# GRU and block attention on one core: the order of the first transfers, and how the bias and the constants get in

## The reference

```python
def cell(h, x):                       # 64 times; h [32, 512]
    gi = x @ W_ih + b_ih              # [32, 1536]
    gh = h @ W_hh + b_hh
    r = sigmoid(i_r + h_r); z = sigmoid(i_z + h_z)
    n = tanh(i_n + r * h_n)
    return (1 - z) * n + z * h
x = x + gru(cond, x)                  # [32, 64, 512]
blocks = x.reshape(32, 8, 8, 512).sum(2)
keys = rms_norm(blocks @ Wk.T) * rms_weight
attn = softmax(keys @ cond[1])
out = layernorm(x + (attn @ blocks) @ Wo.T) * ln_gamma + ln_beta
x = x + out
```

## Time and profile before

| | us |
|---|---|
| median of 3 runs | 377.51 (377.33 to 377.56) |
| the profiled execution | 377.32 |
| its span | 375.5 |
| TensorE busy | 362.8 (97%) |
| VectorE busy | 261.3 (70%) |
| ScalarE busy | 159.3 (42%) |
| GpSimd busy | 21.6 (6%) |

### The profile page before, as it was taken

The page is one execution under the profiler, slowest core; times in us unless marked ns, Lnnn a source line. Parts: engine busy times, 40 slices in busy tenths (PEclk is TensorE's granted clock), DMA queues, the critical chain, the costliest instruction groups (busy, mean ns, idle before and its releaser), DMA issues.

```text
span 375.5 us, 9832 instructions
## 1 busy us (share of the span) xinstructions
PE 362.8 (97%) x3285; PEld 213.5 (57%) x3285; DVE 261.3 (70%) x1132; ACT 159.3 (42%) x506; POOL 21.6 (6%) x55
## 2 busy tenths in 40 slices
PE   7999999999999999999999999999999999997894
PEld 4465555665655566666555666655556666334562
DVE  3725667777676778686768767676778676778785
ACT  4702226262534344352526262534344464756210
POOL 7002000000000000000000000000000000100230
PEclk9999999999999999999999999999999999999998
DMA  5975535323232322324141323232332322110047
GB/s 180 404 295 120 162 96 158 100 70 100 73 98 70 90 62 64 98 57 111 43 105 41 98 70 98 70 98 70 84 79 59 92 61 81 38 42 21 11 172 276
DMA packets 27485, 38.64 MB, mean 103 GB/s; under 512 B 2988, under 2 KB 19016, under 8 KB 27464
## 3 DMA queue, kind: packets, MB, share of 16 engines
q1 hardware_dynamic: 27432, 38.36, 35.4%
q10 hardware_dynamic: 32, 0.01, 0.0%
HBM read 18.17 MB, written 4.19 MB: 60 GB/s over the span
## 4 chain that ended last, share of the span: by engine, by line
PE 89%; DVE 6%; POOL 1%; issue 1%; DMA 1%; ACT 0%; DVEq 0%; POOLq 0%; SPq 0%
PE gates_ps L607 43%; PE gi_ps L575 37%; DVE gcx L1098 1%; POOL w_hh L376 1%; PE first_ps L607 1%; PE first_ps L668 1%; PE fourth_ps L607 1%; PE third_ps L607 1%; PE keys_ps L607 1%; PE fourth_ps L668 1%; PE third_ps L668 1%; PE keys_ps L668 1%; DMA h_tok<-hist 1%; DVE w_hh L1021 1%; PE gi_ps L589 1%
## 5 line engine op out<-in xcount | busy, mean ns | idle before, releaser
L607 PE MATMUL gates_ps<-w_hh,turned 128*32 128x384 f32 x1920 | 167.3, 489 | 0.5 <-DVE turned L829 0.5
L607 PEld LDWEIGHTS gates_ps<-w_hh,turned 128*32 128x32 f32 x1920 | 56.4, 109 | 85.5 <-issue 56.5
L575 PE MATMUL gi_ps<-w_ih_hi,xt_hi 128*128 128x384 f32 x240 | 87.2, 363 | 0.0
L575 PE MATMUL gi_ps<-w_ih_hi,xt_lo 128*128 128x384 f32 x240 | 81.2, 338 | 0.0
L575 PE MATMUL gi_ps<-w_ih_lo,xt_hi 128*128 128x384 f32 x240 | 80.2, 334 | 0.0
L489 ACT ACTIVATE rz<-gates_ps 128x256 f32<-128x256 f32 x60 | 23.1, 385 | 128.9 <-PE gates_ps L607 128.8
L893 DVE TENSOR_TENSOR rz<-gates_ps,rz 128x128 f32<-128x128 f32 x60 | 17.5, 292 | 79.6 <-ACT rz L489 79.6
L575 PEld LDWEIGHTS gi_ps<-w_ih_hi,xt_hi 128*128 128x128 f32 x240 | 45.0, 187 | 37.5 <-issue 36.9
L575 PEld LDWEIGHTS gi_ps<-w_ih_lo,xt_hi 128*128 128x128 f32 x240 | 45.1, 188 | 0.0
L575 PEld LDWEIGHTS gi_ps<-w_ih_hi,xt_lo 128*128 128x128 f32 x240 | 45.0, 187 | 0.0
L829 DVE STREAM_TRANSPOSE turned<-hist 128x32 f32<-128x32 f32 (+1 forms) x192 | 36.7, 216 | 2.2
(11 more groups left out here) (221 smaller groups left out, 302.5 us busy)
## 6 DMA issues: line engine op xcount, KB each, us to landing
gi<-gi_tok SPq DMA_DIRECT2D x60, 192.0 KB, 3.4
x1t<-in_x_t_dram SPq DMA_DIRECT2D x16, 256.0 KB, 3.1
gcx<-in_x_tok_dram SPq DMA_DIRECT2D x16, 256.0 KB, 3.2
h_tok<-hist SPq DMA_DIRECT2D x64, 64.0 KB, 2.2
out_dram<-gcx SPq DMA_DIRECT2D x16, 256.0 KB, 2.2
gcx<-in_w_ih_dram SPq DMA_DIRECT2D x4, 768.0 KB, 7.5
w_hh<-in_w_hh_dram SPq DMA_DIRECT2D x4, 768.0 KB, 8.9
wo_t<-in_wo_t_dram SPq DMA_DIRECT2D x1, 1024.0 KB, 5.4
```

The source lines that it names most:

```text
L575: mm = pe.matmul(gi_ps[tok][:, 0:G3], a[:, k, :], w[:, k, gi_cols(j)], start=(k == 0 and a is xt_hi and w is w_ih_hi), stop=(k == NJ - 1 a ...
L607: mm = pe.matmul(gates_bank(t)[j * B:(j + 1) * B, P:], before[:, k * B:(k + 1) * B], chunk(w_hh, k, j), start=False, stop=(k == NJ - 1), s ...
```

## The change

The three bias transfers, the four constant transfers, the selection matrices, the layout matmuls and the copies after them are gone. x and W_ih's first quarter are SP's first transfers, without a wait. Third is one broadcast transfer of the bias into all partitions: its source pattern is [4 chunks, 32 copies, 768 values], its destination [128 partitions, 768]. h0 comes after W_ih's last quarter, and x of the next four steps before it. VectorE adds the two biases of r and z, and then adds the bias to each of the four banks in PSUM when TensorE has finished the first quarter's matmuls there (`first_laid`); TensorE's second quarter waits for each bank (`first_seeded`). Seven warming matmuls stand where three stood. gamma, cond's row and rms_weight come in three broadcast transfers behind `b_hh_rz`; GpSimd forms the products `wq` and `wq_rec`. The gi chunk before step 0 takes its lo parts of W_ih last (`lo_last`), with a wait for each quarter, and `split_x` comes before the last quarter. The transpose of beta goes from step 0 to step 3. The copy of wq after step 0 is gone. `br_all` and `br_t` are one block smaller.

```diff
+                if last:
+                    sp.wait_ge(wq_ready, 2)
...
-            sp.wait_ge(bias_made, 1)
-            sp.dma_start(bias_rows[0:NJ, 0:G3], b_ih_d).then_inc(bias_in, 16)
-            sp.dma_start(bias_rows[NJ:2 * NJ, P:3 * P], b_hh_d[0:2 * D].rearrange("(j n) -> j n", j=NJ)
-                         ).then_inc(bias_in, 16)
-            sp.dma_start(bias_rows[NJ:2 * NJ, 3 * P:], b_hh_d[2 * D:].rearrange("(j n) -> j n", j=NJ)
-                         ).then_inc(bias_in, 16)
             sp.dma_start(x1t[:, 0], x_t_d[:, 0:NJ, :]).then_inc(x_first_in, 16)
             load_w_ih(0)
-            sp.dma_start(hist[:, S - 1, :], cond_d).then_inc(h0_in, 16)
+            sp.dma_start(bias_in_rec, bias_d[:, None, :].broadcast_to([NJ, B, 6 * P])).then_inc(bias_in, 16)
             load_w_ih(1)
             load_w_ih(2)
+            load_x_t(1)
             load_w_ih(3)
-            load_x_t(1)
+            sp.dma_start(hist[:, S - 1, :], cond_d).then_inc(h0_in, 16)
...
+            sp.dma_start(recs[:].rearrange("p c u -> p (c u)"), recs_d[:, None, :].broadcast_to([NJ, B, 4 * P])
+                         ).then_inc(consts_in, 16)
+            sp.dma_start(tok_consts[:].rearrange("p c n -> p (c n)"), rows_d[None, 0:2 * D].broadcast_to([P, 2 * D])
+                         ).then_inc(consts_in, 16)
+            sp.dma_start(rms_tok, rows_d[None, 2 * D:].broadcast_to([P, D])).then_inc(consts_in, 16)
             move_gi(0, -1)
...
+            pool.wait_ge(consts_in, 48)
+            pool.tensor_tensor(wq, wq, rms_tok, ALU.mult).then_inc(wq_ready, 1)
+            pool.tensor_tensor(wq_rec, wq_rec, rms_rec, ALU.mult).then_inc(wq_ready, 1)
...
-            act.activation(bias_rec, first_ps[0][:], ACT.Copy).then_inc(bias_kept, 1)
-            act.wait_ge(bias_kept, 1)
-            act.wait_ge(pe_warmed, Q)
-            for t in (1, 3):
-                act.activation(first_ps[t][:], bias_rec, ACT.Copy).then_inc(first_seeded, 1)
             for k in range(NJ):
+                if k == NJ - 1:
+                    act.wait_ge(pe_warmed, Q + 1)
+                    split_x(1)
                 act.wait_ge(w_ih_in[k], 16)
                 act.activation(w_ih_hi[:, k, :], w_stage[:, k, :], ACT.Copy).then_inc(w_hi_ready, 1)
...
+                order = [(k, a, w) for k in range(NJ) for a, w in terms]
+                if lo_last:
+                    order = [(k, a, w) for a, w in (terms[0], terms[2], terms[1]) for k in range(NJ)]
+                for m, (k, a, w) in enumerate(order):
+                    if lo_last and w is w_ih_lo:
+                        pe.wait_ge(w_lo_ready, k + 1)
...
-                if first and s == 0:
-                    lay_pick(small_ps, 2)
...
-            keep_warm(2)
-            pe.wait_ge(pick_made, 4)
-            pe.wait_ge(bias_in, 48)
-            pe.matmul(first_ps[0][:], own_rows, bias_rows, start=True, stop=True).then_inc(bias_laid, 1)
-            pe.wait_ge(pick_made, 5)
-            pe.wait_ge(wq_row_ready, 1)
-            pe.matmul(gi_ps[0][:, 0:3 * P], own_rows, const_rows[:, 0:3, :], start=True, stop=True
-                      ).then_inc(consts_laid, 1)
-            lay_pick(gi_ps[1], 0)
-            keep_warm(1).then_inc(pe_warmed, 1)
+            keep_warm(7).then_inc(pe_warmed, 1)
...
                 for t in range(Q):
-                    if k == 0 and t == 0:
-                        pe.wait_ge(bias_kept, 1)
-                    if k == 0 and t == 1:
-                        pe.wait_ge(first_seeded, Q - 1)
+                    if k == 1:
+                        pe.wait_ge(first_seeded, t + 1)
                     for j in range(NJ):
...
+                    if k == 0:
+                        mm.then_inc(first_laid, 1)
...
-            dve.memset(const_rows, 0.0).then_inc(rows_made, 1)
-            dve.memset(bias_rows, 0.0).then_inc(bias_made, 1)
...
-            dve.tensor_copy(first_ps[2][:], bias_rec).then_inc(first_seeded, 1)
+            dve.wait_ge(bias_in, 16)
+            dve.tensor_tensor(bias_rec[:, P:3 * P], bias_rec[:, P:3 * P], bias_in_rec[:, D:], ALU.add
+                              ).then_inc(bias_summed, 1)
+            dve.wait_ge(bias_summed, 1)
+            for t in range(Q):
+                dve.wait_ge(first_laid, t + 1)
+                dve.tensor_tensor(first_ps[t][:], first_ps[t][:], bias_rec, ALU.add).then_inc(first_seeded, 1)
+            split_w(0)
+            split_w(1)
+            split_x(1)
+            split_w(2)
             dve.wait_ge(h0_in, 16)
             for c in parts:
                 dve.transpose(turned[:, S - 1, c], hist[:, S - 1, c]).then_inc(ht_ready, 1)
-            for k in range(NJ):
-                split_w(k)
-            split_x(1)
+            split_w(3)
```

More of the change, by code:

```diff
@@ L66, in gru_block_attention @@
         scalar_warm = sb("scalar_warm", [P, 1])
[L68 to L71, removed]
+        tok_consts = sb("tok_consts", [P, 2, D])
+        gamma_tok, wq = tok_consts[:, 0, :], tok_consts[:, 1, :]
+        recs = sb("recs", [P, 4, P])
+        gamma_rec, beta_rec, wq_rec, rms_rec = (recs[:, c, :] for c in range(4))
         beta_t = sb("beta_t", [P, P])
@@ L314, in _ @@
         def _(pool):
[L315 to L324, removed]
             pool.memset(ident[:], 0.0).then_inc(made, 1)
@@ L503, in step @@
                 quad = i * 2 + s // Q - 1
-                if peeled and s == 0:
-                    act.wait_ge(consts_laid, 3)
-                    act.activation(wq[:], small_ps[:], ACT.Copy).then_inc(consts_kept, 1)
+                if peeled and s == S - 1:
                     act.wait_ge(beta_turned, 1)
@@ L639, in keep_warm @@
                 return mm
-            def lay_pick(bank, c):
-                for j in range(NJ):
-                    mm = pe.matmul(bank[:, j * P:(j + 1) * P], pick[:, j, :], const_rows[:, c, :],
-                                   start=True, stop=True)
-                mm.then_inc(consts_laid, 1)
-            keep_warm(2)
-            pe.wait_ge(pick_made, 4)
-            pe.wait_ge(bias_in, 48)
-            pe.matmul(first_ps[0][:], own_rows, bias_rows, start=True, stop=True).then_inc(bias_laid, 1)
-            pe.wait_ge(pick_made, 5)
-            pe.wait_ge(wq_row_ready, 1)
-            pe.matmul(gi_ps[0][:, 0:3 * P], own_rows, const_rows[:, 0:3, :], start=True, stop=True
-                      ).then_inc(consts_laid, 1)
-            lay_pick(gi_ps[1], 0)
-            keep_warm(1).then_inc(pe_warmed, 1)
+            keep_warm(7).then_inc(pe_warmed, 1)
             pe.wait_ge(x_first_in, 16)
@@ L1138 @@
     b_hh = by_chunk(inputs["L0_cond_b_hh"], (0, 1, 2))[0]
+    b_ih = by_chunk(inputs["L0_cond_b_ih"], (2, 0, 1)).reshape(NJ, G3)
+    rms, gamma, beta = (inputs[f"L1_cond_{name}"] for name in ("rms_weight", "ln_gamma", "ln_beta"))
     laid_out = {
@@ L1144 @@
         "w_ih": by_chunk(inputs["L0_cond_W_ih"], (2, 0, 1)).reshape(D, 3 * D), "w_hh": inputs["L0_cond_W_hh"],
-        "b_ih": by_chunk(inputs["L0_cond_b_ih"], (2, 0, 1)).reshape(NJ, G3),
-        "b_hh": _np.concatenate([b_hh[:, 0:2].reshape(-1), b_hh[:, 2].reshape(-1)]),
-        "rms_weight": inputs["L1_cond_rms_weight"],
+        "b_ih": b_ih,
+        "b_hh_rz": b_hh[:, 0:2].reshape(-1),
+        "bias": _np.concatenate([b_ih, b_hh[:, 2], b_hh[:, 0], b_hh[:, 1]], axis=1),
+        "recs": _np.concatenate([a.reshape(NJ, P) for a in (gamma, beta, cond[1], rms)], axis=1),
+        "rows": _np.concatenate([gamma, cond[1], rms]),
         "wk_t": inputs["L1_cond_Wk"].transpose(1, 0), "wo_t": inputs["L1_cond_Wo"].transpose(1, 0),
-        "gamma": inputs["L1_cond_ln_gamma"], "beta": inputs["L1_cond_ln_beta"],
     }
```

78 lines of the change are left out of this document (28 added, 50 removed).

## The result

Beside each other on one chip, the changed kernel took 383.21 us (median of 6 runs, 381.19 to 384.84), the kernel before 377.75 (6 runs, 377.33 to 378.43): a ratio of 1.0142 with a 95% interval of [1.0121, 1.0162]: slower. The forecast was 376.8 with a range of 374.8 to 378.2: the sign was wrong. The profiled execution took 382.63 us, of which the span is 380.6, 5.1 longer than before.

A forecast was written before the change was run, and what follows sets the result against it. TensorE's unbroken matmul run was taken as the bound, with matmuls and bytes as equal walls at the start. +0.15 for step 0 and -0.89 for `lay_pick` gave -0.74 us: 376.8 us, range 374.8 to 378.2.

The forecast's parts named there:

- Earlier first transfers: At the start: x and all transfers go out 2.55 us earlier, and TensorE begins real work at 6.6 instead of 9.38.
- The bias broadcast: Ahead of w_ih's second quarter: four DMA engines carry 98.3 KB each at 25.4 GB/s, 3.87 us, delaying later transfers on them.
- The clock: Rival: TensorE's idling before w_ih's second quarter drops its clock to half; +2.0 us, 379.5 in all; chance 0.08.
- the straggler: Rival: the slowest DMA engine at the start is one of the bias's four; w_hh lands at 25.4, 378.0 us; chance 0.12.
- +0.15 for step 0: End of step 0: w_hh's last quarter lands at 24.2, so the step ends at 25.1 against 24.93; matmul wall alike.
- Removed `lay_pick`: Between step 0's chunk and step 1: this matmul work leaves the chain, -0.89 us, whole.
- Bias adds hidden: VectorE's bias sum and four PSUM adds, 3.2 us, end before TensorE's second quarter needs them; cost 0, hidden by 1.5 us.
- Constants at no cost: Constants queued behind b_in and b_hh_rz, 1.05 MB, end near 32.7, first wanted in step 3; cost 0, cover 1.5 us.
- b_in is late: Rival: constants mix with b_in before step 1; each 1 us beyond the cover costs up to 1 us; 379; chance 0.07.
- The rival of sixteen engines: At the start: sixteen engines carry the bias in 0.97 us, step 0 ends 1.58 earlier, -2.47 in all, 375.0; chance 0.20.

## Why the prediction was wrong

- **Earlier first transfers: right.** x went out at 0.74 (forecast 0.71), w_ih's first quarter was in by 5.6 (5.5). TensorE began at 5.91, sooner than my 6.6, and was done with the first quarter at 8.73, not 9.6, since the full clock came during the warming. That made the idle stretch longer.
- **The bias broadcast: the step that failed, by size.** The engine count was right: four. The price was not. The prediction took 98.3 KB on each of four engines at 25.4 GB/s, 3.87 us; measured were 12.27 - 5.58 = 6.7 us from w_ih's first quarter to VectorE's sum. Two things were assumed and untrue. First, that an engine with more rows keeps its rate: alone, four engines in blocks of 32 partitions moved 21 GB/s each, and 15.5 beside the other transfers. Second, that the twelve others don't notice: all sixteen together moved 233 GB/s at a share of 0.92. So w_ih's second quarter came at 13.95, not 12.1.
- **The clock: a rival with chance 0.08, and it happened.** Its mechanism was right: TensorE idled 5.22 us. A mean of 0.98 over 5 to 12 us is a half clock for the last 0.2 to 0.3 of them, so the clock had been full for some 3 us of idling when it fell, much as at the end of the kernel before. It cost 2.3 us, against 2.8 forecast; in the four other executions where it fell in this place (two engines, distinct rows, VectorE's additions, blocks of eight) the same stretch cost 1.6, 1.7, 2.6 and 3.0. The chance hung on the transfer's rate, which I had taken as certain: the 2.5 us of forecast idling were only 0.6 less than what had come before the fall in rows 8, and only the straggler was allowed to lengthen them.
- **+0.15 for step 0: measured +4.27**, 2.01 from the late quarter and 2.3 from the clock. w_hh's last quarter was no wall any more, because the matmuls were later than it.
- **Removed `lay_pick`: right**, -0.90 against -0.89.
- **Bias adds hidden: right in the change**, although the cover shrank: with the bias at 12.27, bank 0's addition was over at 13.4, 0.5 us before TensorE could use it. With four transfers in blocks of eight the additions were what TensorE waited for.
- **Constants at no cost: right in the change, for the wrong reason.** It seems to hold there because everything else is late. With sixteen engines, b_in mixed with the constants and cost 1.2 us: the mechanism of the rival "b_in is late".
- **Not seen:** GpSimd's additions now ran beside the state update of step 0 (0.64), 0.40 at the loop's first return, and 0.7 in the end phase, where the granted clock is 0.58 in 349:353. The last shows up in some other kernels' executions too, also in one with a fast start (constants issued in step 2), and neither in the one with warming matmuls nor in the one with VectorE's additions to the change. So it isn't shown to belong to the change; its cause stays open, as does that of the 0.40.
- **The rival of sixteen engines** gave 375.0 for a kernel that measured 376.89; it had the gain of the start (step 1 3.10 us earlier, 2.47 forecast) and lacked the b_in stall.

What stays open: why few engines beside the full streams drop to 15 to 17 GB/s and slow the rest. That their rows cross the parts of SBUF that the other engines are writing would fit the two runs with blocks of eight partitions, and two engines at 25.5 GB/s alone, but beside the streams four blocks of eight gained only some 1.5 us. Which share is whose wasn't separated.

## What to carry to other kernels

Here a broadcast whose pattern began with four went over four DMA engines, one with two over two, and the weights behind it came late (13.95 and 19.21); with 32 or 128 first they came at 9.6 to 9.7. So give both sides a first dimension that is a multiple of 16, as a larger tensor in DRAM or as several transfers. Where TensorE waits early for a landing, price the clock as well as the wait: here 2.01 us of lateness brought 2.3 us of half clock. Before constants are moved behind a critical transfer, ask what waits for the last byte of that transfer, and put them after it by program order in time, not by place in the queue.

## What the runs showed of the hardware

- With nothing else in flight, four DMA engines in blocks of 32 partitions moved 85 GB/s, two in blocks of 64 moved 51, and four in blocks of eight 96 (one execution each, and the first read four rows again and again, the others 128 rows). The engine count alone doesn't give the rate.
- While a transfer on four engines was in flight, all sixteen together moved 233 GB/s from 5 to 12 us in place of 395, at nearly full share: the share of busy time hides it, GB/s shows it.
- GpSimd additions from SBUF made two pairs of VectorE operations, 0.28 and 0.34 us with the additions elsewhere, last 0.70 and 0.85.
